# Constants loaded first, the last store halved, and k turned into rows of tokens by VectorE and small transfers instead of TensorE

## What is computed

```python
def _L0_attn_ref(x, Wq, Wk, Wv, Wo):            # 16 heads of 16
    q, k, v = elu(x @ Wq.T) + 1, elu(x @ Wk.T) + 1, x @ Wv.T
    def step(carry, qkv):
        kv_sum = kv_sum + einsum('bhd,bhe->bhde', k_i, v_i)
        k_sum = k_sum + k_i
        out_i = einsum('bhd,bhde->bhe', q_i, kv_sum) / (sum(q_i * k_sum) + EPS)
    ...
    return out @ Wo.T
def _L0_ffn_ref(...):                            # 8 experts and a shared one
    scores = sigmoid(x @ gate_w.T)               # 2 of 4 groups, then the best 4 experts
    ...
    y = einsum('eni,eih->enh', silu(g) * u, Wd)
    return einsum('enh,ne->nh', y, cw) + _mlp(x, Wg_s, Wu_s, Wd_s)
x = x + _L0_attn_ref(_layernorm(x), ...)
x = x + _L0_ffn_ref(_layernorm(x), ...)
```

## Time and profile before

| | us |
|---|---|
| three runs: median (lowest to highest) | 1095.8 (1094.74 to 1096.29) |
| the profiled execution | 1093.38 |
| its span | 1091.6 |
| TensorE busy in the span | 1048.1 |
| VectorE busy | 875.0 |
| GpSimd busy | 440.4 |
| ScalarE busy | 430.6 |
| one step of the repeated list | 65.4 |

### The profile page before, as it was taken

How to read it: one execution, slowest core, us unless ns; L and a number is a source line. 1 busy time by engine, 2 the same in 40 slices (tenths; PEclk the granted TensorE clock), 3 DMA queues, 4 the chain that set the end, 5 groups by cost and what they waited for, 6 DMA issues and landing times.

```text
span 1091.6 us, 22588 instructions
## 1 busy us (share of the span) xinstructions
PE 1048.1 (96%) x8688; PEld 907.7 (83%) x8688; DVE 875.0 (80%) x1826; ACT 430.6 (39%) x781; POOL 440.4 (40%) x366
## 2 busy tenths in 40 slices
...
DMA packets 38073, 56.89 MB, mean 52 GB/s; under 512 B 3280, under 2 KB 20432, under 8 KB 37968
## 3 DMA queue, kind: packets, MB, share of 16 engines
q1 hardware_dynamic: 37968, 55.45, 16.5%
...
## 4 chain that ended last, share of the span: by engine, by line
PE 88%; DVE 8%; issue 2%; ACT 1%; DMA 1%; SPq 0%; DVEq 0%; ACTq 0%
PE bank L795 47%; PE y_bank L795 19%; PE bank L893 6%; PE bank L907 6%; PE bank L840 3%; PE bank L921 2%; PE bank L934 1%; DVE den L694 1%; DVE den L693 1%; PE bank L937 1%; DVE compare L692 1%; PE bank L880 1%; DMA wr_raw<-in_w_router 1%; PE bank L873 1%; DVE rden L695 1%
## 5 line engine op out<-in xcount | busy, mean ns | idle before, releaser
L588 POOL TENSOR_TENSOR h_lo<-et,h_hi 128x512 fp32r<-128x512 f32 x144 | 185.2, 1296 | 320.4 <-ACT h_hi L550 320.4
L584 POOL TENSOR_TENSOR et<-et,cw_all 128x512 f32<-128x512 f32 x128 | 165.5, 1308 | 227.8 <-DVE et L781 201.8
L795 PE MATMUL bank<-xt_hi,wg_hi 128*128 128x512 f32 x576 | 232.0, 403 | 1.9 <-DVE et L775 1.9
L795 PE MATMUL bank<-xt_hi,wg_lo 128*128 128x512 f32 x576 | 228.0, 396 | 0.0
L795 PE MATMUL bank<-xt_lo,wg_hi 128*128 128x512 f32 x576 | 227.4, 395 | 0.0
L550 ACT ACTIVATE h_hi<-et 128x512 fp32r<-128x512 f32 x144 | 90.2, 627 | 230.1 <-PE y_bank L795 125.7
L685 DVE TENSOR_TENSOR scores<-bank,cst 128x512 f32<-128x512 f32 x256 | 165.7, 680 | 13.8 <-PE bank L893 12.6
L795 PE MATMUL y_bank<-wd_hi,h_hi 128*128 128x256 f32 x576 | 166.2, 289 | 0.0
L795 PE MATMUL y_bank<-wd_hi,h_lo 128*128 128x256 f32 x576 | 161.0, 280 | 0.0
L795 PE MATMUL y_bank<-wd_lo,h_hi 128*128 128x256 f32 x576 | 160.6, 279 | 0.0
L541 ACT ACTIVATE et<-bank 128x512 f32<-128x512 f32 x144 | 85.6, 596 | 133.8 <-PE bank L795 123.9
...
## 6 DMA issues: line engine op xcount, KB each, us to landing
cw_all<-cw_dram SPq DMA_DIRECT2D x128, 256.0 KB, 3.9
x_in<-in_x SPq DMA_DIRECT2D x16, 512.0 KB, 5.3
out_y<-x_mid SPq DMA_DIRECT2D x16, 512.0 KB, 3.4
scores<-in_w_gate_up SPq DMA_DIRECT2D x4, 512.0 KB, 8.8
cw_all<-in_w_qkvo SPq DMA_DIRECT2D x2, 512.0 KB, 5.5
x_mid<-in_w_down SPq DMA_DIRECT2D x1, 512.0 KB, 9.8
cw_all<-in_w_down SPq DMA_DIRECT2D x1, 512.0 KB, 3.5
...
```

The source lines that it names most:

```text
L584: nc.gpsimd.tensor_tensor(et[:, i % ET, :], et[:, i % ET, :], cw_all[:, (i - 1) % CW, :], ALU.mult)\
L588: nc.gpsimd.tensor_tensor(h_lo[:, i % HR, :], et[:, i % ET, :], h_hi[:, i % HR, :].bitcast(f32), ALU.subtract).then_inc(h_lo_done, 1)
L795: ins = nc.tensor.matmul(dst, l, r, start=first and n == 0, stop=last and n == 2, skip_group_check=shared)
```

## The change

1. k is turned without TensorE. VectorE transposes `kf` in blocks of 32 by 32 into `k_blocks` (one instruction, 128x384), and SP issues 16 transfers of 32 partitions x 3 x 128 bytes (12 KB) that carry the blocks to their partitions in `k_tok`. There is one `k_blocks` for both halves: `k_turn.1` waits until the transfers of `k_move.0` have landed. `state` waits for its `k_move`. TensorE's three transposes, ScalarE's copy and the use of a bank go.
2. `consts` is issued second. `power` (-0.5) is set by GpSimd rather than loaded. The first `ln1_apply` is done by VectorE. TensorE makes 16 transposes that nobody reads before its first task.
3. The store is issued in two halves, and `result` starts its first half when half of the last `down` is there (`half_done`).
4. The comparison tiles of the router are shared, with the same number of instructions.
5. All lists and `BANK` are written anew.

The repeated lists of TensorE, VectorE and SP, and the first ones of VectorE and SP:

```diff
     "PE": """
-        up.5.3 wo.1.2 wo.0.2 gate.6.3 down.0.3 scores.1.1 down.1.3 down.2.3 up.6.3 gate.7.3 gate.8.3 state.1.1
-        down.3.3 turn.2.2 turn.3.2 up.7.3 up.8.3 down.4.3 scores.2.1 values.0.1 values.1.1 router.0.2
-        inter.0.1 down.5.3 inter.1.1 scores.3.1 turn.1.0 turn.0.0 down.6.3 gate.0.2 gate.2.2 q.0.0 up.2.2
-        k.0.0 down.7.3 up.0.2 gate.1.2 k.1.0 k_turn.0.0 values.2.1 values.3.1 weights_turn.0.2 scores.0.0
-        up.1.2 inter.2.1 inter.3.1 q.1.0 k_turn.1.0 v.1.0 gate.4.2 down.8.3 v.0.0 up.4.2 up.3.2 gate.3.2
-        gate.5.2 state.0.0
+        up.5.3 down.0.3 wo.0.2 wo.1.2 down.1.3 scores.1.1 gate.6.3 gate.8.3 down.2.3 gate.7.3 turn.2.2 up.8.3
+        up.6.3 down.3.3 turn.3.2 down.4.3 up.7.3 scores.2.1 values.0.1 values.1.1 inter.0.1 inter.1.1
+        state.1.1 router.0.2 turn.0.0 turn.1.0 down.5.3 up.0.2 scores.3.1 gate.0.2 down.6.3 k.0.0 q.0.0 v.1.0
+        k.1.0 q.1.0 values.2.1 values.3.1 weights_turn.0.2 inter.2.1 down.7.3 inter.3.1 gate.1.2 gate.2.2
+        up.2.2 up.1.2 gate.3.2 scores.0.0 down.8.3 v.0.0 gate.4.2 gate.5.2 up.3.2 state.0.0 up.4.2
         """,
     "DVE": """
-        wo.1.2 wo.0.2 ln2_stats.0.2 mask.6.1 mask.4.1 gate.6.3 mask.7.1 ln2_apply.0.2 mask.5.1 up.6.3
-        state.1.1 gate.7.3 up.7.3 gate.8.3 turn.2.2 up.8.3 turn.3.2 ln1_stats.0.0 mask.9.1 mask.8.1 router.0.2
-        mask.10.1 spread.0.1 mask.11.1 mult.0.1 mask.15.1 mask.12.1 mask.13.1 turn.1.0 turn.0.0 mask.14.1
-        gate.0.2 route.0.2 gate.2.2 rank0.0.2 q.0.0 up.0.2 up.2.2 k.0.0 rank1.0.2 gate.1.2 k.1.0 cum.0.0
-        mask.1.0 mask.3.0 spread.1.1 mask.2.0 mask.0.0 cum.1.0 mult.1.1 up.1.2 at.0.1 q.1.0 result.0.3 den.0.0
-        den.1.0 at.1.1 gate.4.2 up.4.2 gate.3.2 gate.5.2 state.0.0 up.3.2 up.5.2
+        wo.1.2 wo.0.2 ln2_stats.0.2 mask.5.1 mask.6.1 gate.6.3 ln2_apply.0.2 mask.4.1 mask.7.1 turn.2.2 up.6.3
+        gate.8.3 up.8.3 turn.3.2 gate.7.3 ln1_stats.0.0 mask.10.1 up.7.3 mask.9.1 mask.8.1 mask.11.1 state.1.1
+        spread.0.1 router.0.2 mult.0.1 turn.0.0 turn.1.0 route.0.2 mask.13.1 mask.15.1 mask.14.1 spread.1.1
+        mask.12.1 gate.0.2 up.0.2 rank0.0.2 k.0.0 rank1.0.2 cum.0.0 k.1.0 q.0.0 cum.1.0 mult.1.1 at.0.1 q.1.0
+        gate.2.2 gate.1.2 up.2.2 up.1.2 den.1.0 mask.2.0 mask.0.0 k_turn.0.0 den.0.0 mask.1.0 mask.3.0
+        k_turn.1.0 result.0.3 gate.4.2 gate.3.2 at.1.1 up.3.2 up.4.2 gate.5.2 up.5.2 state.0.0
         """,
     "SP": """
-        load_x.0.0 cw_store.0.2 cw_load.1.2 cw_load.3.2 cw_load.0.2 store.0.3 cw_load.5.2 cw_load.4.2
-        cw_load.2.2 cw_load.7.2 cw_load.6.2
+        load_x.0.0 cw_store.0.2 cw_load.3.2 cw_load.2.2 cw_load.0.2 cw_load.1.2 cw_load.5.2 k_move.0.0
+        k_move.1.0 cw_load.4.2 store.0.3 cw_load.6.2 cw_load.7.2
         """,
 }
...
     "DVE": """
-        ln1_stats.0.0 piece.0.0 piece.1.0 ln1_stats.0.1 turn.0.0 turn.1.0 k.0.0 cum.0.0 q.0.0 k.1.0 q.1.0
-        den.0.0 mask.1.0 mask.0.0 mask.2.0 cum.1.0 mask.7.0 mask.6.0 turn.1.1 mask.4.0 mask.3.0 state.0.0
-        turn.0.1 mask.5.0 state.1.0 den.1.0 mask.11.0 mask.8.0 mask.10.0 mask.9.0 spread.0.0 k.0.1 mult.0.0
-        cum.0.1 mask.15.0 mask.13.0 q.0.1 mask.14.0 k.1.1 mask.12.0 spread.1.0 at.0.0 q.1.1 cum.1.1 mult.1.0
-        mask.1.1 mask.0.1 mask.3.1 den.0.1 at.1.0 mask.2.1 state.0.1 den.1.1
+        ln1_stats.0.0 ln1_apply.0.0 piece.0.0 piece.1.0 turn.0.0 turn.1.0 ln1_stats.0.1 k.0.0 k_turn.0.0
+        cum.0.0 k.1.0 k_turn.1.0 q.0.0 q.1.0 den.0.0 mask.1.0 mask.0.0 mask.3.0 mask.2.0 mask.5.0 mask.6.0
+        spread.0.0 state.0.0 mask.7.0 mask.4.0 turn.0.1 turn.1.1 cum.1.0 mask.9.0 mask.8.0 mask.11.0 mask.10.0
+        den.1.0 k.0.1 q.0.1 spread.1.0 state.1.0 k_turn.0.1 mult.0.0 cum.0.1 mask.14.0 mask.15.0 k.1.1
+        mask.13.0 mask.12.0 den.0.1 mult.1.0 q.1.1 cum.1.1 mask.1.1 k_turn.1.1 mask.2.1 mask.3.1 at.0.0
+        mask.0.1 at.1.0 state.0.1 den.1.1
         """,
     "SP": """
-        load_x.0.0 piece.0.0 piece.1.0 load_x.0.1 piece.2.0 piece.3.0 piece.4.0 piece.5.0 consts.0.0 piece.7.0
-        piece.8.0 piece.9.0 piece.6.0
+        load_x.0.0 consts.0.0 piece.0.0 piece.1.0 piece.2.0 load_x.0.1 piece.3.0 piece.4.0 piece.5.0 piece.6.0
+        k_move.0.0 piece.7.0 k_move.1.0 piece.8.0 k_move.0.1 k_move.1.1 piece.9.0
         """,
```

The code (an "..." stands for what is left out):

```diff
+        power = sb("power", [P, SUBS])[:, :]
...
         q_half = sb("q_half", [P, KC, 2, S])
+
+        k_blocks = sb("k_blocks", [P, (SUBS - 1) * P])
         k_tok = sb("k_tok", [P, KC, SUBS - 1, P])
...
+        k_blocked, K_BLOCKED = sem("k_blocked"), nth("DVE", ("k_turn",))
+        k_moved, K_MOVED = sem("k_moved"), nth("SP", ("k_move",), 16 * 16)
...
+                elif name == "k_move":
+
+                    sp.wait_ge(k_blocked, K_BLOCKED["k_turn", i, b])
+                    wait_filled(sp, "state", i, b - 1)
+                    for g in range(4):
+                        for a in range(4):
+                            src = k_blocks[32 * g:32 * g + 32, :].rearrange("t (c a e) -> t c a e", c=SUBS - 1, a=4)
+                            sp.dma_start(k_tok[32 * a:32 * a + 32, i, :, 32 * g:32 * g + 32], src[:, :, a, :])\
+                                .then_inc(k_moved, 16)
-                    sp.wait_ge(y_drained, Y_DRAINED["result", 0, b])
-                    sp.dma_start(out_v[b], x_mid[b % 2][:, :, :]).then_inc(out_sent[b % 2], 16)
+                    for j in range(2):
+                        half = slice(j * HALF, (j + 1) * HALF)
+                        sp.wait_ge(y_drained, Y_DRAINED["result", 0, b] - 1 + j)
+                        sp.dma_start(out_v[b][:, half, :], x_mid[b % 2][:, half, :]).then_inc(out_sent[b % 2], 16)
...
-                elif name == "k_turn":
-                    act.wait_ge(filled, FILLED["k_turn", i, b])
-                    wait_filled(act, "state", i, b - 1)
-                    nc.scalar.activation(k_tok[:, i, :, :].rearrange("p c d -> p (c d)"),
-                                         bank[BANK["k_turn", i]][:, 0:(SUBS - 1) * P], ACT.Copy)\
-                        .then_inc(drained[BANK["k_turn", i]], 1)
...
+            nc.gpsimd.memset(power, -0.5).then_inc(zeros_set, 1)
             nc.gpsimd.memset(v_win[:, :, :, 1, :], 0.0).then_inc(zeros_set, 1)
-            pool.wait_ge(small_in, 48)
+            pool.wait_ge(zeros_set, 1)
...
-                    if b == 0:
-                        dve.wait_ge(small_in, 48)
                     nc.vector.tensor_scalar(minus_mean[:, :], m_sum[:, :], -0.5, None, ALU.mult)\
                         .then_inc(var1_ready, 1)
                     dve.wait_ge(var1_ready, VAR1["ln1_stats", 0, b])
+                elif name == "ln1_apply":
+
+                    dve.wait_ge(shift_ready, SHIFT["rstd1", 0, b])
+                    for s in range(SUBS):
+                        last = nc.vector.tensor_scalar(norm1[:, s, :], x_in[b % XB][:, s, :], rstd1[:, s:s + 1],
+                                                       shift1[:, s:s + 1], ALU.mult, ALU.add)
+                    last.then_inc(norm1_ready, 1)
+                    dve.wait_ge(small_in, 48)
...
+                elif name == "k_turn":
+                    dve.wait_ge(drained[BANK["k", i]], USES["k", i, b])
+                    wait(dve, k_moved, K_MOVED, "k_move", 1 - i, b if i == 1 else b - 1)
+                    nc.vector.transpose(k_blocks[:, :], kf[:, i, 0:(SUBS - 1) * P]).then_inc(k_blocked, 1)
...
-                    dve.wait_ge(down_done, DOWN["down", SLOTS - 1, b])
                     for j in range(2):
+                        if j == 0:
+                            dve.wait_ge(half_done, b + 1)
+                        else:
+                            dve.wait_ge(down_done, DOWN["down", SLOTS - 1, b])
                         xm = x_mid[b % 2][:, 2 * j:2 * j + 2, :]
                         nc.vector.tensor_tensor(xm, xm, y_bank[j][:, :, :], ALU.add).then_inc(y_drained, 1)
...
             pe.wait_ge(small_in, 48)
+            for n in range(WARM):
+                nc.tensor.transpose(bank[BANK["turn", 0]][:, 0:P], ident, ident)
...
+                        if i == SLOTS - 1 and s == HALF - 1:
+                            last.then_inc(half_done, 1)
...
-                elif name == "k_turn":
-                    pe.wait_ge(drained[BANK["k", i]], USES["k", i, b])
-                    for c in range(SUBS - 1):
-                        last = nc.tensor.transpose(bk[:, c * P:(c + 1) * P], kf[:, i, c * P:(c + 1) * P], ident)
-                    last.then_inc(filled, 1)
                 elif name == "state":
-                    pe.wait_ge(drained[BANK["k_turn", i]], USES["k_turn", i, b])
+                    pe.wait_ge(k_moved, K_MOVED["k_move", i, b])
```

More of the change, by code:

```diff
@@ L25 @@
 BANKS = 6
+WARM = 16
 BEGIN, END = 2, B
@@ L39 @@
         """,
     "ACT": """
[L41 to L44, removed]
+        split.3.3 gate.6.3 split.5.3 wide.1.1 turn.2.2 split.4.3 gate.8.3 turn.3.2 gate.7.3 split.6.3
@@ L45 @@
```

(30 more changed lines are left out.)

128 lines of the change are left out of this document (63 added, 65 removed).

## The result

| | before | after |
|---|---|---|
| median (lowest to highest), us | 1095.27 (1093.36 to 1096.29) | 1318.53 (1307.29 to 1325.22) |
| profiled execution / span, us | 1093.38 / 1091.6 | 1317.74 / 1316.0 |
| mean step over 12 steps, us | 65.3 | 80.7 |

The ratio is 1.203, with an interval of 1.1945 to 1.2116: slower by a fifth. The span grew by 224 us; fourteen steps at 15.4 us more are 216 of them. So the question is what a step does with 15 us.

What follows compares the result with a forecast made beforehand. TensorE bounds the steps, VectorE the start. From the profiled 1093.4 us, +42 for fourteen steps of 68.5 instead of 65.45, -5 start, -1 end: 1129; as a median 1131 us, given range 1070 to 1155.

Steps and rivals of the forecast that it cites:

- TensorE's own work in a step: TensorE's step without the k transposes (0.66 us) and a stall behind VectorE (0.36 us): 65.45 falls to 64.4 us.
- a: When VectorE ends the first k transpose, counted from T: 3.3 us, or 4.5 if GpSimd holds up a denominator; 3.9 taken.
- T: Time zero of the walk through a step: the start of `scores.0.0` on TensorE.
- D: Time from the finished transpose to the last of 16 landings: 15 issues plus 1.4 us, 7.4 us (6.2 to 8.6).
- stall from D: TensorE's wait each step, at `up.5` behind VectorE's queue, for the late landing: 4.05 us (2.25 to 5.85).
- the stall behind VectorE: TensorE's existing stall before the task after `state.0`, 1.03 against 0.67 us: 0.36 us a step, expected to go.
- S: TensorE's stall in every step, a + D - 7.25: 4.05 us, bounds 2.25 and 5.85.
- VectorE's queue behind `k_turn.1`: Drains queued behind the waiting second transpose delay TensorE's `up.5` to 14.4 us instead of 10.35, overlapping the wait before `state`.
- The start: Before the steps: first large product at 14 instead of 24.75 us, first mask at 31.8 instead of 37.68; gain 5 us.
- The end: After the last `down`: first add beside its last half (0.6 us), half the last store's data (up to 0.8); gain 1.
- Packets: Rival: 1536 packets of 128 bytes per `k_move` set the limit; D near 11, +92 us, 1181 us; chance 0.04.
- Cheap transfers: Rival: on-chip issues cost a third of the rows, so the wait is covered; 1073 us (1068 to 1085); chance 0.23.

Runs made afterwards that it cites:

- e11: The kernel before with the new end alone: store in two halves, first add of result started by half_done; 1088.52 us, ratio 0.9937.

## Why the prediction was right in sign and wrong in size

| term | predicted | measured |
|---|---|---|
| TensorE's own work in a step | 64.4 | 64.5 |
| a, first transpose done after T | 3.9 | 3.2, in five of 14 steps 4.3 |
| one issue, start to start | 0.40 (0.32 to 0.48) | 0.64 |
| D | 7.4 (6.2 to 8.6) | 11.4 |
| stall from D | 4.05, behind VectorE | 6.5, before `state` |
| the store behind 32 issues | 0, otherwise 1 to 2 | 4.2 |
| slower clock after the stalls | not in the sum | 5.3 |
| step | 68.5 | 80.5 |

- **Right:** that TensorE sets the step, its own work, that the issues can't be hidden, and the form of D, 15 issues and one landing (1.8 us, 1.4 taken). So the change is slower. In the own work two errors cancel in part: the transposes were worth 0.44 us (64.95 to 64.5) and not 0.66, and the stall behind VectorE 0.45 and not 0.36, but in nine of fourteen steps only.
- **The issue's price.** This mis-sized term is the root. I bounded it with 0.32 and 0.48, from issues with DRAM on one side; no row of before had both ends in the on-chip memory. I went near 0.32 because that row had 32 partitions. What makes the price isn't settled. It isn't the kind of source and destination alone: the stores of `k_blocks` to DRAM have the kind of that row and took 0.62. Nor is it the transfer alone: the very transfer of that row, the 16 KB of the routing weights, takes 0.32 us in the changed kernel and 0.58 in the one with the moves early, where it stands right behind sixteen issues (start, us):

```profile
427.84 0.32 SPq L429 DMA_DIRECT2D cw_dram<-cw_t  x1
```

```profile
549.23 0.60 SPq L446 DMA_DIRECT2D k_tok<-k_blocks  x1
549.87 0.58 SPq L429 DMA_DIRECT2D cw_dram<-cw_t  x1
```

  An upper bound from rows of another shape and another place in the queue is no bound. At 0.64 my own formula gives S = 3.2 + 11.4 - 7.25 = 7.35 us and, with the rest of the sum as it stands, about 1178; that is the size of the wait but not yet of the result.
- **The store costed at nothing.** I saw that the store stands behind `k_move.1` and traced only `cw_load.4` to who wants it. I didn't ask who waits for the store: `wo` on VectorE, which writes the same `x_mid`, and TensorE behind it. The store put between (with `cw_load.4`) shows that it is worth nearly half of the loss: 99 of 223 us. This is the step that failed worst.
- **a.** 3.2 us in the step shown, just below my 3.3 to 4.5, and 4.3 in five of the fourteen steps. It hangs on one instruction of the first denominator. In every one of these steps but one it starts within 0.05 us of the end of one GpSimd product, with the next right behind. In the step shown it is short, in the next one it takes what it took in the earlier trace rows:

```profile
436.05 1.28 POOL L593 TENSOR_TENSOR et<-et,cw_all 128x512 f32<-128x512 f32 x1 [1.65 <-DVE et L800]
437.29 0.18 DVE L713 TENSOR_SCALAR den<-den 128x32 f32<-128x32 f32 x1
```

```profile
517.82 1.32 DVE L713 TENSOR_SCALAR den<-den 128x32 f32<-128x32 f32 x1
```

  The rule of the Trainium skill ("SBUF — State Buffer", section "SBUF: two separate sides"), by which a was 4.5, agrees with the five long ones, which took 1.32 to 1.33 us, about as long as one product. In eight steps the instruction took 0.18 us and the product beside it ran on; why these got in first no row shows. The mean of a is 3.6.
- **The clock.** This term was missing from the sum. I priced a stall at its length. Here 10.7 us of stall bring 5.3 more, as the products after each run at half rate until the clock is back. With the store in its place the mean clock is 0.94, with one transfer 0.99, in the kernel after 0.92.
- **Where the wait sits.** I took VectorE's queue behind `k_turn.1` for the later of two waits. Moving it changed nothing. VectorE was in fact ready as forecast, 3.0 us after the landing (3.1 taken), but TensorE at half clock needed 3.8 us for `state` and `up.4` instead of 2.1, and so came later than VectorE. That is read from the one step above.
- **The start.** The first large product at 13.95 came as said (14), but the first mask did not:

```profile
31.82 0.58 DVE L693 STREAM_TRANSPOSE k_blocks<-kf 128x384 f32<-128x384 f32 x1 [8.57 <-DMA k_tok<-k_blocks]
...
37.87 3.86 DVE L704 TENSOR_TENSOR scores<-bank,cst 128x512 f32<-128x512 f32 x6 [0.71 <-PE bank L915]
```

  The second transpose was put at 26.8 and stood at 31.8, by the same D; the 5 us gained are the 5 us lost, and the first mask is where it was (37.68 in the earlier trace rows). With one transfer it comes at 28.66.
- **The end.** 1.3 us in e11, 1 predicted; the gain in the steps was missed, though the stall it removes was in the earlier trace rows.
- **The rivals.** "Packets" came nearest in time (1181) by a cause that is wrong. "Cheap transfers" is what the kernel with one transfer is: 1084, not 1073, since the new lists and start save less than I gave them: the mean of 12 steps is 64.70 us against 65.27, 0.57 us a step and not 1.05. The rule of the Trainium skill ("DMA: Bandwidth & Descriptors", section "Rules for kernel authors") to gather small transfers into one was right here: one instead of sixteen is worth 234 us (without the exchange), five by way of DRAM instead of sixteen 109 us (with it).

The cause of the 223 us is shown by runs: number of issues, place of the store. What sets the price of an issue stays open. The split of the step into stall and clock is read from one profiled execution.
